# Feed-forward block behind a cross attention on one Trainium2 core: in the product stage 1,024 instead of 512 token rows only as magnitudes, and three gate chunks rounded by VectorE

## The reference

```python
def act_qdq(x):                      # 16 bits, one scale for the whole tensor
    qmax = 2.0 ** (ACT_BITS - 1) - 1.0
    scale = jnp.maximum(jnp.max(jnp.abs(x)) / qmax, 1e-12)
    return jnp.clip(jnp.round(x / scale), -qmax - 1.0, qmax) * scale
x = act_qdq(x)
up = act_qdq(x @ lpbq_dequant(w_up).T)
gate = act_qdq(x @ lpbq_dequant(w_gate).T)
sig = fixed_qdq_u16(jax.nn.sigmoid(gate))
gate = act_qdq(gate * sig)
o = act_qdq(gate * up)
return o @ lpbq_dequant(w_down).T
```

## Time and profile before

| | us |
|---|---|
| three runs | 1139.15, 1139.65, 1142.57 (median 1139.65) |
| the profiled execution | 1142.61 |
| its span in the profile | 1140.8 |
| granted TensorE clock, mean over the span | 0.983 of full |
| busy: PE | 1078.3 (95%) |
| busy: DVE | 1010.0 (89%) |
| busy: ACT | 602.9 (53%) |
| busy: POOL | 38.0 (3%) |

### The profile page before, as it was taken

One profiled execution on the slowest core, in us unless ns is written; L12 is line 12 of the kernel. 1 busy time (PEld: TensorE's weight loads), 2 busy tenths in 40 slices (PEclk: granted clock), 3 DMA queues, 4 the chain that ended last, 5 costly groups with the idle time before them and its releaser, 6 DMA issues.

```text
span 1140.8 us, 20540 instructions
## 1 busy us (share of the span) xinstructions
PE 1078.3 (95%) x8360; PEld 504.3 (44%) x8360; DVE 1010.0 (89%) x1416; ACT 602.9 (53%) x706; POOL 38.0 (3%) x42
## 2 busy tenths in 40 slices
PE   5999999999999999999999999999999998999359
PEld 3443344434443444344434443444333332788258
DVE  7687988898989898999998899988899999889986
ACT  3555545454545555555555545554555455347763
POOL 0500000000000000000000000000000000003200
PEclk9999999999999999999999999999999999899779
DMA  8001300010001000100010001000000000000002
GB/s 268 16 20 25 121 20 20 20 39 20 20 20 38 20 20 20 39 19 20 20 39 20 21 16 42 20 20 11 29 29 20 20 29 11 1 1 1 1 1 74
DMA packets 37861, 34.57 MB, mean 30 GB/s; under 512 B 14210, under 2 KB 28739, under 8 KB 37511
## 3 DMA queue, kind: packets, MB, share of 16 engines
q1 hardware_dynamic: 37766, 33.26, 9.4%
HBM read 30.75 MB, written 2.36 MB: 29 GB/s over the span
## 4 chain that ended last, share of the span: by engine, by line
PE 81%; DVE 12%; issue 4%; ACT 2%; DMA 0%; POOLq 0%; POOL 0%; DVEq 0%; ACTq 0%
PE ps L1480 27%; PE ps L1496 27%; PE ps L1343 5%; PE ps L1408 4%; PE ps L1353 4%; PE ps L1361 4%; PE ps L1630 3%; PE ps L1694 3%; DVE acc L974 2%; PE ps L1372 1%; DVE e_buf L1071 1%; DVE fst L858 1%; DVE gt L1237 1%; ACT e_buf L688 1%; PE ps L1332 1%
## 5 line engine op out<-in xcount | busy, mean ns | idle before, releaser
L688 ACT ACTIVATE e_buf<-ps 128x1024 f32<-128x1024 f32 x400 | 410.7, 1027 | 310.3 <-PE ps L1480 303.4
L1496 PE MATMUL ps<-e_buf,vb 64*64 64x512 f32 x3072 | 401.2, 593 | 4.7 <-DVE e_buf L1071 4.6
L974 DVE TENSOR_TENSOR acc<-acc,e_buf 128x1024 f32<-128x1024 f32 x318 | 386.4, 1215 | 0.0
L1071 DVE TENSOR_SCALAR e_buf<-e_buf 128x1024 f32<-128x1024 f32 x400 | 272.8, 682 | 53.6 <-ACT e_buf L688 52.2
L1496 PEld LDWEIGHTS ps<-e_buf,vb 64*64 64x64 f32 x3072 | 111.7, 133 | 221.3 <-issue 187.3
L1480 PE MATMUL ps<-qb,kb_odd 64*64 64x512 f32 x1600 | 208.7, 589 | 0.0
L1480 PE MATMUL ps<-qb,kb_even 64*64 64x512 f32 x1600 | 208.6, 589 | 0.0
L1480 PEld LDWEIGHTS ps<-qb,kb_odd 64*64 64x64 f32 x1600 | 61.5, 133 | 109.8 <-issue 109.6
L1480 PEld LDWEIGHTS ps<-qb,kb_even 64*64 64x64 f32 x1600 | 61.3, 133 | 110.2 <-issue 110.1
L1060 DVE TENSOR_TENSOR xacc<-ps,xacc 128x512 f32<-128x512 f32 x60 | 41.1, 689 | 35.5 <-PE ps L1408 35.1
L1630 PE MATMUL ps<-hT,wgu 128*128 128x512 f32 x276 | 64.9, 396 | 0.0
(11 more groups left out here) (177 smaller groups left out, 796.2 us busy)
## 6 DMA issues: line engine op xcount, KB each, us to landing
ebc<-el_rows SPq DMA_DIRECT2D x64, 128.0 KB, 2.9
rden<-inv_rows SPq DMA_DIRECT2D x62, 128.0 KB, 2.8
xacc<-in_x_dram SPq DMA_DIRECT2D x4, 512.0 KB, 7.4
wst<-in_L_xattn_Wkv_dram SPq DMA_DIRECT2D x16, 128.0 KB, 2.7
out_dram<-z SPq DMA_DIRECT2D x7, 256.0 KB, 2.1
wst<-in_L_xattn_Wq_dram SPq DMA_DIRECT2D x8, 128.0 KB, 2.8
wo_raw<-in_L_xattn_Wo_dram SPq DMA_DIRECT2D x8, 128.0 KB, 3.0
acc<-in_ctx_dram SPq DMA_DIRECT2D x2, 512.0 KB, 7.4
```

The costliest lines, as they stand in the source:

```text
L688: nc.scalar.activation(e_buf[:, g % E_BUFS, :, :], sc[:, g % 2, :, :], ACT.Exp, scale=float(DH) ** -0.5).then_inc(exp_done, 1)
L974: dve.tensor_tensor(acc[:, t0 % 3, :, :], a, e_buf[:, tiles_to(t0, st) % E_BUFS, :, :], ALU.add).then_inc(summed, 1)
L1071: dve.tensor_scalar(tile, tile, EXP_LO, EXP_HI, ALU.max, ALU.min).then_inc(clip_done, 1)
L1496: ins = pe.matmul(ps_o[DH * h:DH * h + DH, half, :], vb[rows, p % 2, st, DH * h:DH * h + DH], e_buf[rows, g % E_BUFS, h, :], start=(st == ...
```

## The change

`LATE` goes from block 3 to block 2: the two last blocks, 1,024 rows, are treated as the last one was. Six chunks instead of nine get a signed product and a `top`; six instead of three go through the custom instruction. POOL's two roundings go, and ACT rounds all twelve chunks of up. DVE itself rounds gate chunks 0, 2 and 4 of the order (`GI_VECTOR`, by `product_gates`), so ACT rounds nine. In the fourth stage g = 4 to 7 are made from signed integers, so ACT issues twelve `signed_integers`, in a new placement, and `out_integers(4)` and `(5)` wait for the first six, `(6)` and `(7)` for all twelve. Gate's signed integers are written over the front half of their own source in `gt`, so `result` has no wait for `z` any more. `ohl` and `oi` change places in memory, so that blocks 2 and 3 of `up` survive.

```diff
-LATE = NBS - 1
-BY_BLOCK = [e for e in range(FCH) if e % NBS != LATE] + [e for e in range(FCH) if e % NBS == LATE]
-SIGNED = FCH - FCH // NBS
-SIGNED_AT = {2: (0, 1, 2), 3: (3, 4), 4: (5,)}
+LATE = NBS - 2
+BY_BLOCK = [e for e in range(FCH) if e % NBS < LATE] + [e for b in range(LATE, NBS) for e in range(FCH) if e % NBS == b]
+SIGNED = FCH // NBS * LATE
+SIGNED_AT = {1: (0, 1), 2: (2, 3, 4), 3: (5, 6), 4: (7, 8, 9), 5: (10, 11)}
+GI_VECTOR = (0, 2, 4)
...
-            sb("pad2", [P, (2 * KT * N - FT * N // 2)], stack=ffn)
-            ohl_rows = sb("ohl_rows", [P, 4, N], F32R, stack=ffn)
-            ohl = ohl_rows[:, :, 0:FT * DM].rearrange("p (g i) (f d) -> p g i f d", g=2, f=FT)
             oi = sb("oi", [P, 2, FT, DM], I16, stack=ffn)
+            sb("pad2", [P, (2 * KT * N - FT * N // 2 - FT * DM)], stack=ffn)
+            ohl_rows = sb("ohl_rows", [P, FT, N], F32R, stack=ffn)
+            ohl = ohl_rows[:, :, 0:4 * DM].rearrange("p f (g i d) -> p g i f d", g=2, i=2)
...
-        g_signed = zf[:, 2 * FC:2 * FC + FT * NB // 2].bitcast(I16).rearrange("p (f n) -> p f n", f=FT)
+        g_signed = [gt[:, :, NB * b:NB * b + NB // 2].bitcast(I16) for b in range(LATE, NBS)]
...
# POOL, end of its program
-            pool.wait_ge(scale_done, 3)
-            for e in range(2):
-                pool.tensor_scalar(chunk(ui, e), chunk(up, e), fsc[:, 2, 2:3], 1.0, ALU.mult, ALU.mult).then_inc(ui_pool, 1)
...
# ACT, stage three
-                if n >= 2:
-                    nc.scalar.activation(chunk(ui, e), chunk(up, e), form, scale=fsc[:, 2, 2:3]).then_inc(ui_done, 1)
+                nc.scalar.activation(chunk(ui, e), chunk(up, e), form, scale=fsc[:, 2, 2:3]).then_inc(ui_done, 1)
+                if n in GI_VECTOR:
+                    continue
...
# ACT, signed_integers(n)
-                f = n // 2 * 2
+                late, part = divmod(n, FT)
+                f, e = part // 2 * 2, BY_BLOCK[SIGNED + n // 2]
                 act.wait_ge(o_done, FCH)
-                if n % 2 == 0:
-                    ins = nc.scalar.activation(g_signed[:, f:f + 2, :], chunk(gt, BY_BLOCK[SIGNED + n // 2]), ACT.Copy, scale=fsc[:, 3, 2:3])
+                if part % 2 == 0:
+                    ins = nc.scalar.activation(g_signed[late][:, f:f + 2, :], chunk(gt, e), ACT.Copy, scale=fsc[:, 3, 2:3])
...
# DVE, stage three
+            def product_gates(n):
+
+                if n >= GI_BUFS:
+                    dve.wait_ge(o_done, n + 1 - GI_BUFS)
+                dve.tensor_scalar(gi_at(n), chunk(gt, BY_BLOCK[n]), fsc[:, 3, 2:3], None, ALU.mult).then_inc(gi_first, 1)
+
+            product_gates(0)
             for n, e in enumerate(BY_BLOCK):
-                dve.wait_ge(gq_done, n + 1)
-                await_ui(dve, n)
+                if n in GI_VECTOR:
+                    dve.wait_ge(gi_first, GI_VECTOR.index(n) + 1)
+                else:
+                    dve.wait_ge(gq_done, n + 1 - sum(1 for v in GI_VECTOR if v < n))
+                dve.wait_ge(ui_done, n + 1)
...
                     ins = top(fst[:, 4, 2 * last:2 * last + 2], chunk(gt, last))
+                if n + 1 in GI_VECTOR:
+                    product_gates(n + 1)
...
# DVE, out_integers(g)
                 if DM * g >= NB * LATE:
-                    dve.wait_ge(signed_done, FT)
-                    n0 = DM * g - NB * LATE
-                    dve.scalar_tensor_tensor(out=oi[:, g % 2, :, :], in0=g_signed[:, :, n0:n0 + DM], scalar=fsc[:, 4, 2:3],
+                    late, n0 = g // 2 - LATE, DM * (g % 2)
+                    dve.wait_ge(signed_done, FT * (late + 1))
+                    dve.scalar_tensor_tensor(out=oi[:, g % 2, :, :], in0=g_signed[late][:, :, n0:n0 + DM], scalar=fsc[:, 4, 2:3],
...
# DVE, result(g)
-                if g >= GROUPS // 2:
-                    dve.wait_ge(oi_done, GROUPS + 1)
```

More of the change, by code:

```diff
@@ L333, in attention_ffn @@
         y_last_ready, y_last_taken = sem("y_last_ready"), sem("y_last_taken")
+        gi_first = sem("gi_first")
         h_tail, signed_done, last_top = sem("h_tail"), sem("signed_done"), sem("last_top")
@@ L340, in attention_ffn @@
         gi_done, sig_done, su_done = sem("gi_done"), sem("sig_done"), sem("su_done")
-        gs_done, gq_done, ui_done, ui_pool, o_done = sem("gs_done"), sem("gq_done"), sem("ui_done"), sem("ui_pool"), sem("o_done")
+        gs_done, gq_done, ui_done, o_done = sem("gs_done"), sem("gq_done"), sem("ui_done"), sem("o_done")
         oi_done, o_high, o_low = sem("oi_done"), sem("o_high"), sem("o_low")
@@ L393, in gi_by_scalar @@
             return e % 3 == 2
[L395 to L400, removed]
         @block.sync
@@ L791, in signed_integers @@
             def signed_integers(n):
-                f = n // 2 * 2
+                late, part = divmod(n, FT)
+                f, e = part // 2 * 2, BY_BLOCK[SIGNED + n // 2]
                 act.wait_ge(o_done, FCH)
-                if n % 2 == 0:
-                    ins = nc.scalar.activation(g_signed[:, f:f + 2, :], chunk(gt, BY_BLOCK[SIGNED + n // 2]), ACT.Copy, scale=fsc[:, 3, 2:3])
+                if part % 2 == 0:
+                    ins = nc.scalar.activation(g_signed[late][:, f:f + 2, :], chunk(gt, e), ACT.Copy, scale=fsc[:, 3, 2:3])
                 else:
-                    e = BY_BLOCK[SIGNED + n // 2]
                     ins = nc.scalar.activation(chunk(ui, e), chunk(up, e), ACT.Copy, scale=fsc[:, 2, 2:3])
```

## The result

The change makes the kernel slower: 1147.4 us median of six runs (1145.8 to 1149.1) against 1141.0 us of the kernel before on the same chip (six runs), ratio 1.0055, 95% interval 1.0042 to 1.0069. The forecast was +3.7 us; measured is +6.4 us. The direction and both stalls came as forecast; the size did not, and 1147.4 lies outside the stated range.

What follows compares the result with a forecast made beforehand. The prediction took VectorE to bound stage three and PE stage four. Terms -1.86 and +5.56 gave +3.7 us: 1142.61 to 1146.3 us profiled, or 1139.65 to 1143.4 us as median, range 1140.8 to 1146.9.

Steps and rivals of the forecast that it cites:

- both stalls: Stage four: PE waits before groups 3 and 5, losing 2.26 and 3.30 us, 5.56 us in total.
- the order fault: Stage four: low parts 3 and 5 wait behind products needing integers placed after high parts 3 and 5.
- The slack of 0.52 us in front of group 3: Stage four before the change: group 3's operands are ready at 1116.35 us, PE needs them at 1116.87.
- the hand-over: Stage four: VectorE's product starts 0.03 us behind the end of the signed integer it waits for.
- Nothing lost, by a hair: Stage four, group 4: operands ready at 1123.20 us, PE busy until 1123.33, so no loss.
- the gain of stage three: Three top fewer on VectorE, 3.40 us, minus 1.54 for gate roundings: 1.86 us gained, between 1.14 and 2.06.
- product 1 eats what GpSimd's leaving gives: Start of stage three: product 1 waits for ScalarE's third instruction, so removing GpSimd's roundings gains zero.
- The port rule: Start of stage three: VectorE and GpSimd take turns at shared ports, so removing GpSimd's work would return 0.83 us.
- The sum, -1.86 + 5.56: Whole kernel: stage three's gain plus stage four's stalls make +3.7 us.
- the fall of the clock behind the longer stall: Rival, stage four: the idle time before group 5 also halves PE's clock, +1.8 us, total 1145.2; chance 0.18.
- PE's clock-keeping (3.99 us) hangs on the eleventh product and just moves: End of stage three: the 3.99 us of clock-keeping follow the eleventh product and only shift in time.
- a difference of 3.0 us between the profiled execution and the median: Whole kernel: the profiled execution lies 3.0 us above the median of three runs; carried over to the forecast.

Runs made afterwards that it cites:

- e2: The changed kernel with clock-keeping matmuls on PE in the two gaps, ahead of the waits for groups 3 and 5; 1145.2 us, ratio 1.0034.
- e4: e1 with the signed integers re-placed: sixth behind high part 2, only the eleventh and twelfth still behind high part 5; 1144.3 us, ratio 1.0028.
- e6: e5 without gate chunks on VectorE, so only the 512 further rows remain of stage three's change; 1137.0 us, ratio 0.997.
- e7: e1 with all 24 roundings on ScalarE, none on VectorE or GpSimd; stage three 26.22 us in one profiled execution.
- e12: The kernel before, with only PE's clock-keeping released by the tenth product instead of the eleventh; 1137.5 us, ratio 0.998.
- e1: The changed kernel with the twelve signed integers placed earlier on ScalarE, four of them ahead of the first high part; 1140.5 us, ratio 0.9991.
- e8: e1 with low part 1 issued ahead of integers 2 on VectorE; 1139.0 us, ratio 0.9972.
- e9: e6 with low part 1 issued ahead of integers 2 on VectorE; 1136.4 us, ratio 0.9962.
- e11: The changed kernel once more, unaltered; 1148.2 us, ratio 1.0064 to the kernel before.
- e10: e9 with PE's clock-keeping before the last spread released by the tenth product instead of the eleventh; 1136.9 us, ratio 0.9963.
- e3: The kernel before, with only its sixth signed integer moved from behind high part 4 to behind high part 5; 1143.9 us, ratio 1.0027.
- e5: e1 with GpSimd rounding up's first two chunks again; stage three 24.57 us in one profiled execution.

## Why the prediction was right and wrong

**Right: what bounds each stage, and the order fault.** The slack of 0.52 us in front of group 3, the place of the sixth and the twelfth integer and the two stalls were read from the trace before. Forecast 2.26 and 3.30 us, measured without the clock 2.37 and 3.43 (e2). The misses of 0.1 each lie in the hand-over: VectorE's product starts 0.13 to 0.15 us behind the end of the integer that it waits for (e2), where 0.03 was assumed. "Nothing lost, by a hair" for group 4 held, too.

**Right: the gain of stage three** (1.86 forecast, 1.78 measured; from the first `top` to the last read-out 19.74 us, forecast about 19.6), and that product 1 eats what GpSimd's leaving gives. The port rule that I set against the row would have given 0.83 us; the changed trace shows product 0 back at 1.23 us and product 1 waiting 0.78 us.

**Wrong: the clock, and this is the step that failed.** The sum, -1.86 + 5.56, has no term for it. The text put the fall of the clock behind the longer stall into a rival with a chance of 0.18 and a price of 1.8 us, argued "it is shorter than the one that shows a fall", and gave the shorter stall no chance of it at all. The runs show the fall behind both, 1.5 to 1.6 us each, 3.1 in sum (after against e2), in both profiled executions. One row at 4.62 us of idle time says that this length is enough; it says nothing about where it stops being enough. I took the one example as the limit.

The Trainium skill, "TensorE: Matmul & The Clock Gate", section "HAM oscillation — how this bites in real kernels", was cited in the prediction as pointing to better odds for this case, and the traces of after agree that an idle gap between groups of matmuls returns the clock to half rate. Its own example has waits of about 3 to 5 us, though, so it is no support for a fall behind the stall of 2.10 us, which the trace shows as well; and behind the 3.22 us of e4 the clock did not fall.

The sum with both falls is -1.8 (stage three) + 5.8 (both stalls) + 3.1 (both falls) + 0.3 (the varying piece, 7.37 against 7.08): +7.4, and the tail grew by 7.45. Between the medians it is 6.4 us, between the medians of the three lower runs of each 7.3.

**Half wrong: "PE's clock-keeping (3.99 us) hangs on the eleventh product and just moves".** It moves (and took 4.21 us), but I then took the last maximum as the end of the stage. As long as VectorE paces the last products the two are 1.0 us apart and it makes no difference; e6 and e7 show that it does when the pace changes, and e12 that the release of the clock-keeping is the bound. The gain held because VectorE paces the last products before and after, so the eleventh moved by the same 1.78 us as the last maximum; the forecast did not see that it depended on this. VectorE's three gate chunks bring nothing: without them and with GpSimd's work (e6) the tail is 0.9 us shorter than with them (e1).

**The scatter of the runs.** I carried a difference of 3.0 us between the profiled execution and the median over without a cause. It has one. The windows around 975 us, of before and then of after, and the output projection of the last head pair on PE in each:

```profile
973.00:974.00 1.00, 1.00 (x9) 1.00 (x8) 1.00 (x2) 0.00 (x0) 0.00 (x0) 0.70 0.00 0
...
975.00:976.00 1.00, 1.00 (x4) 0.73 (x4) 0.04 (x1) 0.00 (x0) 0.00 (x0) 0.50 0.00 0
...
979.00:980.00 1.00, 1.00 (x8) 0.83 (x6) 0.00 (x0) 0.00 (x0) 0.00 (x0) 0.50 0.06 16
```

```profile
975.00:976.00 1.00, 1.00 (x9) 0.80 (x10) 0.77 (x2) 0.00 (x0) 0.00 (x0) 1.00 0.00 0
```

```profile
974.14 3.76 PE L1417 MATMUL ps<-wo_g,oT 128*128 128x256 f32 x8
977.83 3.16 PE L1428 MATMUL ps<-wo_g,oT 64*128 64x256 f32 x16
```

```profile
973.24 1.97 PE L1419 MATMUL ps<-wo_g,oT 128*128 128x256 f32 x8
975.14 2.00 PE L1430 MATMUL ps<-wo_g,oT 64*128 64x256 f32 x16
```

The same 24 matmuls take 6.9 us in one and 4.0 in the other. These 3 us are lost ahead of the part that the change touches, and the runs of the kernel before stand in two groups 3 us apart, 1139.1 to 1139.9 and 1141.6 to 1143.2 (19 and 14 of the 33 beside e1 to e4). Seven of the fourteen traces show this fall (before, e2, e6, e8, e9, e11, e12). Where stage four kept its clock and more than one run was made, the profiled execution lies in the upper group with the fall (before, e2, e6, e8, e9, e12) and in the lower group without it (e1, e4). No experiment held this clock up, so what brings the fall on is open.

## What to carry to other kernels

When work is placed in another engine's order by a table of due times, write down for every consumer the last step behind which its input may stand, and remember that a consumer issued one step ahead of its use needs its inputs one step earlier; here one place too late cost 2.4 us, and the waiting instruction held up a finished one behind it. Where PE runs without a break at a slack of half a microsecond, price each stall twice, once for its length and once for the clock. And look for what the end of a stage really hangs on: a clock-keeping block of 4 us behind the last product but one was the bound, and releasing it one product sooner (e12) or leaving out two of the three parts of stage three's change (e6, e9) did more than the whole change with its order repaired (e1).

## What the runs showed of the hardware that was not expected

- TensorE's granted clock fell to its lower level behind idle stretches of 2.02 us (e10), 2.18 us (e3), 2.10 and 3.23 us (after) and 2.10 and 3.22 us (e11), each time only 0.8 to 1.4 us after PE had started again. It did not behind one of 3.22 us (e4), nor behind those of 0.85 us (after, e1). Length alone does not decide it.
- It also fell, in some executions, at about 973.4 us in the profiled execution of before (mean 0.90 from 973.0 to 973.5, 0.50 from 973.5 on), where PE was busy without a break in the records, from 971.1 us on with matmuls of two columns and then of one column; that costs 3 us. In after the same instructions run and the clock stays at 1.00.
- A float32 to int16 rounding of 1,024 elements on VectorE took 0.75 us alone and 1.53 us beside GpSimd (e5).
- ScalarE wrote int16 over the front half of its own float32 source at the usual 1.14 us, and the wider strides of `ohl` left its 1.48 us and VectorE's 1.76 us as they were (1.47 to 1.48 and 1.75 to 1.76 after).
